# Eleven staging slots for a gathered matrix, and a main loop written out

## The reference

```
XW    = X @ W
s_col = XW @ a[0, :f];  s_row = XW @ a[0, f:]
Z1    = leaky_relu(s_row[:, None] + s_col[None, :], 0.01)
den   = exp(Z1)
num   = A @ den
att   = where(num != 0, den / num, 0)
H     = A @ (att @ XW)
out   = layernorm(X + H)
```

## Time and profile before

| | |
|---|---|
| median of 3 runs | 449.73 us (449.41 to 450.17) |
| profiled execution | 446.65 us |
| its span, first to last instruction | 444.9 us |
| busy in the span | PE 306.8, DVE 280.6, ACT 198.0, POOL 185.5 us |
| mean granted clock of TensorE | 0.843 of full speed |
| loading A, from the first gather to the last matmul of the sums | 57.6 to 186.2 us |
| main loop | 186.5 to about 354 us |
| scatter, second product, layernorm | the rest |

### The profile page before, as it was taken

How to read it: one execution, slowest core, us unless ns; L and a number is a source line. 1 busy time by engine, 2 the same in 40 slices (tenths; PEclk the granted TensorE clock), 3 DMA queues, 4 the chain that set the end, 5 groups by cost and what they waited for, 6 DMA issues and landing times.

```text
span 444.9 us, 5604 instructions
## 1 busy us (share of the span) xinstructions
PE 306.8 (69%) x1466; PEld 145.4 (33%) x1467; DVE 280.6 (63%) x469; ACT 198.0 (45%) x308; POOL 185.5 (42%) x164
## 2 busy tenths in 40 slices
PE   4863214756276456689999999999999720499950
PEld 2563102622123222334434343434344310144420
DVE  0669987277689434499899998966999800201026
ACT  1210030153586233587777787757788820100020
POOL 4000022456878775476455554524555376000000
PEclk9965555886576697999999999999999985699985
DMA  3030042534255566100000000000000041300002
GB/s 117 0 96 2 1 141 71 164 96 122 97 161 158 157 185 196 60 0 1 0 1 0 0 0 0 0 0 0 0 0 1 0 141 47 94 1 0 1 24 71
DMA packets 13439, 24.58 MB, mean 55 GB/s; under 512 B 1648, under 2 KB 8176, under 8 KB 13296
## 3 DMA queue, kind: packets, MB, share of 16 engines
q0 software_dynamic: 5632, 18.88, 13.9%
q1 hardware_dynamic: 7792, 5.50, 4.2%
HBM read 21.23 MB, written 3.15 MB: 55 GB/s over the span
## 4 chain that ended last, share of the span: by engine, by line
PE 49%; DVE 20%; POOL 13%; issue 9%; DMA 5%; ACT 3%; POOLq 0%; SPq 0%; DVEq 0%; ACTq 0%
PE ps L399 17%; PE ps L368 12%; PE ps L428 10%; POOL stage L225 4%; POOL Alo L235 3%; POOL d_b L279 3%; PE ps L394 3%; POOL xws L251 2%; DVE D L574 2%; DMA stage<-adjT,perm 2%; PE ps L301 2%; DVE Alo L744 2%; DVE D L576 2%; PE ps L358 1%; DVE crow L767 1%
## 5 line engine op out<-in xcount | busy, mean ns | idle before, releaser
L269 POOL TENSOR_TENSOR crow<-rrow,cj 128x512 f32<-128x512 f32 x64 | 79.9, 1250 | 76.8 <-DVE crow L767 75.8
L358 PE MATMUL ps<-Ahi,E 128*96 128x512 f16 x128 | 54.6, 484 | 56.3 <-DVE Alo L744 30.0
L399 PE MATMUL ps<-Ahi,D 128*128 x248 | 86.7, 380 | 3.0 <-issue 1.4
L770 DVE TENSOR_TENSOR tmp<-crow,tmp 128x512 f32<-128x512 f32 x64 | 64.4, 1007 | 18.1 <-ACT tmp L508 16.6
L225 POOL DMA_INDIRECT stage<-adjT,perm x32 | 37.3, 1164 | 92.0 <-DVE rs L603 51.8
L368 PE MATMUL ps<-stage,xwp 128*128 128x512 f32 x128 | 70.4, 632 | 1.5 <-DVE stage L757 1.5
L744 DVE TENSOR_TENSOR Alo<-stage,Ahi 128x1024 f16<-128x1024 f32 x24 | 35.5, 1488 | 35.2 <-ACT Ahi L452 35.1
L428 PE MATMUL ps<-Ahi,D 128*128 128x512 f16 x128 | 39.7, 388 | 25.3 <-DVE D L782 25.3
L506 ACT ACTIVATE tmp<-ps 128x512 f32<-128x512 f32 x64 | 38.1, 595 | 37.3 <-PE ps L401 37.3
L452 ACT CAST Ahi<-stage 128x1024 f16<-128x1024 f32 x32 | 33.2, 1042 | 48.2 <-DMA stage<-adjT,perm 47.7
L767 DVE SCALAR_TENSOR_TENSOR crow<-crow 128x512 f32<-128x512 f32 x64 | 49.9, 779 | 0.0
(11 more groups left out here) (158 smaller groups left out, 345.5 us busy)
## 6 DMA issues: line engine op xcount, KB each, us to landing
tmp<-xT SPq DMA_DIRECT2D x1, 1024.0 KB, 4.9
d_xw<-stage SPq DMA_DIRECT2D x1, 1024.0 KB, 5.1
xws<-d_b SPq DMA_DIRECT2D x2, 512.0 KB, 4.7
out<-crow SPq DMA_DIRECT2D x4, 256.0 KB, 2.3
stage<-adjT,perm POOLq DMA_INDIRECT x32, 4.8
xws<-d_xw,perm POOLq DMA_INDIRECT x16, 3.5
d_b<-crow,ranku POOLq DMA_INDIRECT x16, 2.3
stage<-wT SPq DMA_DIRECT2D x1, 64.0 KB, 1.8
```

The source lines that it names most:

```text
L269: nc.gpsimd.tensor_tensor(q_t[c % 2], rrow[:, c * W:(c + 1) * W], cj[:, u:u + 1].to_broadcast([P, W]), ALU.add).then_inc(S["q_ready"], 1)
L358: mm = nc.tensor.matmul(ps[0:R, c, :], E[:, e, b, :], a[:, b, c * W:(c + 1) * W], start=(b == 0 and i == 0), stop=(b == NB - 1 and i == 2))
L399: nc.tensor.matmul(num[c], D[:, d, bass.ds(slot, 1), :], a[:, bass.ds(k, 1), c * W:(c + 1) * W], start=False, stop=(i == 2), skip_group_ch ...
L770: V.tensor_tensor(L_t[c], lz_t[c % 2], L_t[c], ALU.subtract).then_inc(S["sub_done"], 1)
```

## The change

- The ring has eleven slots. Three are in `stage` as before; eight are row blocks 12 to 15 of Ahi and Alo, each read as 1024 float32 columns while it is empty. Gather n + 11 waits for residual n. Casts and residuals from n = 24 on write where slots were, so they wait until the residuals that read those slots are done (`wait_vacated`). The wait for the store of XW moves from the first gather to the eighth.
- Every third residual (n = 2, 5, ..., 29) is POOL's, ten in all, not every fourth.
- The gathers of XW stand at n = 21 to 28, two at each.
- In the main loop POOL does nothing. ACT makes r01 = 0.01 x rrow once, in two instructions; DVE makes the columns shift = -0.99 x score and ebias. The leaky relu is now max(r01 + shift, rrow) in one DVE instruction from two tiles, and the column score goes into the bias of the exp. DVE does it one chunk ahead.
- The loops over pairs are written out on all engines. Only the loop over k is left. The first product of a chunk is split in two halves of 256 columns, the second of which ends the accumulation; the matmul with zeros is gone. PE reads XW directly, and ACT's copies of it (L502) are gone.

```diff
-XWG = 6
-LOS = 4
+XWG = 21
+LOS = 3
+LATE = 12
...
-        st = [stage[:, g * H:(g + 1) * H] for g in range(NG)]
-        q_t = [crow[:, 0:W], crow[:, W:2 * W]]
-        lz_t = [crow[:, 2 * W:3 * W], crow[:, 3 * W:4 * W]]
+        late = [a[:, b, :].bitcast(F32) for b in range(LATE, NB) for a in (Alo, Ahi)]
+        ring = late[1:] + [stage[:, g * H:(g + 1) * H] for g in range(NG)] + late[:1]
+        RG = len(ring)
+        lz_t = [crow[:, i * W:(i + 1) * W] for i in range(2)]
+        r01 = [stage[:, 0:H], crow[:, H:N]]
...
+        def wait_vacated(engine, n, part):
+
+            if n // 2 >= LATE:
+                wait_lo(engine, n // 2 * 2 - (2 if part is Ahi else 3))
...
-            pool.wait_ge(S["xw_out"], 16)
...
-                if n >= NG:
-                    wait_lo(pool, n - NG)
+                if n == RG - NG - 1:
+                    pool.wait_ge(S["xw_out"], 16)
+                if n >= RG:
+                    wait_lo(pool, n - RG)
...
-            for n in range(NG):
+            for n in range(RG):
                 fetch(n)
             for n in range(2 * NB):
                 b, h = divmod(n, 2)
                 if n % LOS == LOS - 1:
                     pool.wait_ge(S["hi_done"], n + 1)
...
+                    wait_vacated(pool, n, Alo)
...
-                if n + NG < 2 * NB:
-                    fetch(n + NG)
+                if n + RG < 2 * NB:
+                    fetch(n + RG)
...
-                if XWG <= n < XWG + NB:
-
-                    for b in range(n - XWG, n - XWG + 1):
+                if XWG <= n < XWG + NB // 2:
+
+                    for b in range(2 * (n - XWG), 2 * (n - XWG + 1)):
...
+            for J in range(NB):
+                lo, hi1 = ends_of(J)
+                for c in range(NC):
+                    t = J * NC + c
+                    if J == 0:
+                        pe.wait_ge(S["sums_sb"], c + 1)
                     else:
-                        lo, hi1 = lo_next, hi1_next
...
+                        pe.wait_ge(S["att_ready"], t - NC + 1)
+                    o = c * W
+                    nc.tensor.matmul(num[c][:, 0:HW], wgt[0:R, J * P:(J + 1) * P], sums[0:R, o:o + HW],
+                                     start=True, stop=False, skip_group_check=True)
+                    with pe.Fori(lo, hi1) as k:
+                        slot = J + (NB - 1) - k
+                        for d, a in ((0, Ahi), (0, Alo), (1, Ahi)):
+                            nc.tensor.matmul(num[c], D[:, d, bass.ds(slot, 1), :], a[:, bass.ds(k, 1), o:o + W],
+                                             start=False, stop=False, skip_group_check=True)
+                    nc.tensor.matmul(num[c][:, HW:W], wgt[0:R, J * P:(J + 1) * P], sums[0:R, o + HW:o + W],
+                                     start=False, stop=True, skip_group_check=True).then_inc(S["num_ready"], 1)
+                    if t >= LAG:
+                        add_bt(t - LAG)
...
-            act.wait_ge(S["xws_in"], 16 * NB)
+            wait_lo(act, 2 * NB - 1)
+            act.wait_ge(S["d_z"], NS)
+            for h in range(2):
+                nc.scalar.mul(r01[h], rrow[:, h * H:(h + 1) * H], SLOPE).then_inc(S["r01_sb"], 1)
             act.wait_ge(S["d_lo"], len(BATCH))
+            act.wait_ge(S["shift_sb"], 2)
...
+            def lz_of(t):
+                J, c = divmod(t, NC)
+                if t < NC:
+                    dve.wait_ge(S["r01_sb"], c // 2 + 1)
+                if t >= 2:
+                    dve.wait_ge(S["sub_done"], t - 1)
+                V.scalar_tensor_tensor(lz_t[t % 2], r01[c // 2][:, c % 2 * W:(c % 2 + 1) * W], shift[:, J:J + 1], rrow[:, c * W:(c + 1) * W],
+                                       ALU.add, ALU.max).then_inc(S["lz_ready"], 1)
```

More of the change, by code:

```diff
@@ L93, in graph_attention_layernorm @@
         a2s = sb("a2s", [P, 2])
-        xwp = sb("xwp", [P, 2, FEAT])
+        shift = sb("shift", [P, NB])
+        ebias = sb("ebias", [P, NB])
         split = sb("split", [P, 2, NB], U32)
@@ L253, in _ @@
                             in_offset=bass.IndirectOffsetOnAxis(ap=perm[:, 1, 2, b:b + 1], axis=0)).then_inc(S["xws_in"], 16)
[L256 to L274, removed]
             for b in range(NB):
@@ L361, in _, with add_bt @@
                     mm.then_inc(S["p_sums"], 1)
-            def add_bt(J, u, c, first, last):
-                t = J * NC + c
+            def add_bt(t):
+                J, c = divmod(t, NC)
                 if c == 0:
-                    pe.wait_ge(S["xwp_ready"], J + 1)
+                    pe.wait_ge(S["xws_in"], 16 * NB)
                 pe.wait_ge(S["att_ready"], t + 1)
-                nc.tensor.matmul(bt[c], xwp[:, u, :], att[c], start=first, stop=last).then_inc(S["bt_added"], 1)
+                nc.tensor.matmul(bt[c], xws[:, J * FEAT:(J + 1) * FEAT], att[c], start=(J == 0), stop=(J == NB - 1)
+                                 ).then_inc(S["bt_added"], 1)
             pe.wait_ge(S["w_lo"], 1)
@@ L372, in _ @@
             LAG = 3
+            HW = W // 2
             def ends_of(J):
[L376 to L405 removed]
@@ L512, in _ @@
-            pair(0, True)
-            with act.Fori(1, NP2) as p:
-                pair(2 * p, False)
-            exp_of(NB * NC - 1, NC - 1)
+                nc.scalar.activation(L_t[c], L_t[c], ACT.Exp, bias=ebias[:, J:J + 1]).then_inc(S["exp_done"], 1)
+            for t in range(NB * NC):
+                c = t % NC
+                act.wait_ge(S["num_ready"], t + 1)
+                if t >= NC:
+                    act.wait_ge(S["att_ready"], t - NC + 1)
+                nc.scalar.activation(L_t[c], num[c], ACT.Square, scale=1.0 / 256).then_inc(S["sq_done"], 1)
+                act.wait_ge(S["sq_done"], t + 1)
+                nc.scalar.activation(L_t[c], L_t[c], ACT.Ln, bias=epst[:, 1:2]).then_inc(S["ln_done"], 1)
+                if t:
+                    exp_of(t - 1)
@@ L754, in att_of @@
+            def att_of(t):
+                c = t % NC
                 dve.wait_ge(S["exp_done"], t + 1)
[L755 removed]
+                if t >= NC:
                     dve.wait_ge(S["bt_added"], t - NC + 1)
                 V.scalar_tensor_tensor(att[c], num[c], 1.0 / 256, L_t[c], ALU.mult, ALU.mult).then_inc(S["att_ready"], 1)
[L759 to L772 removed]
@@ L774, in _ @@
-            pair(0, True)
-            with dve.Fori(1, NP2) as p:
-                pair(2 * p, False)
-            att_of(NB * NC - 1, NC - 1, False)
+            lz_of(0)
+            for t in range(NB * NC):
+                c = t % NC
+                if t + 1 < NB * NC:
+                    lz_of(t + 1)
+                dve.wait_ge(S["lz_ready"], t + 1)
+                dve.wait_ge(S["ln_done"], t + 1)
+                V.tensor_tensor(L_t[c], lz_t[t % 2], L_t[c], ALU.subtract).then_inc(S["sub_done"], 1)
+                if t:
+                    att_of(t - 1)
```

104 lines of the change are left out of this document (24 added, 80 removed).

## The result

The changed kernel takes 432.61 us (median of 4 runs, 432.18 to 432.89) against 449.95 us before in the same session: a ratio of 0.961, interval 0.960 to 0.963. The forecast was 440.8 with a range of 433 to 447: the direction is right, the gain of 17.3 us is almost twice the 8.9 foretold. The profiled execution took 432.18 us, its span is 430.4, 14.5 us under the 444.9 of before. The traces can account for these 14.5; the other 2.8 of the 17.3 come from that the profiled execution of before took 446.65 us where the median is 449.95, and no trace shows where the other executions spend the difference.

A forecast was written before the change was run, and what follows sets the result against it. Loading A was taken as bound by a chain of latencies, the main loop by PE. Span 444.9 - 8.1 + 1.0 - 1.8 = 436.0 us; applied to the median, 449.73 - 8.9 = 440.8 us, range 433 to 447.

The forecast's parts named there:

- Part 1: Loading of A with eleven slots: DMA waits go, copy of crow 3.1 us earlier, batches end at 138.7 us.
- Part 2: End of loading, gathers of XW moved late in POOL's queue: sums end at 178.1 us, a gain of 8.1 us.
- 16 x (0.95 + 0.30) = 20.0: POOL's tail of loading: sixteen gathers of XW at their median, each with a pause, in us; upper end 34.2.
- Rival 3: POOL's tail, sixteen gathers ahead of residual 29, outweighs the rest: slower, 454.5 us; chance 0.07.
- Part 3: Loading, ten residuals on POOL instead of eight: hidden until half block 20, then counted in the tail's sum.
- Part 4: Main loop written out: r01 costs 1.0 us before it, the loop gains 1.8 us, bounds 0 and 4.
- There are two loads per J before and after, so I leave them: 0.: Main loop, PE's step at a new row block: 0.60 us more for two register loads, taken as unchanged.
- Rival 1: Main loop: PE's queue runs ahead when written out, all sixteen stalls go, 9.6 us more, 431.2 us; chance 0.13.
- The sign that was to make Part 4 wrong: Middle of the main loop: a step under 2.4 us, where products 2.48 us apart were foretold.
- The closing matmul with the zero tile took no time on that chain ... : 0: Main loop, end of each chunk's accumulation: replacing that matmul by two halves of 256 columns changes nothing, 0 us.
- Rival 4: Main loop: written-out code stalls in instruction fetch, 9.6 us lost, 450.4 us, no change; chance 0.05.
- Rival 2: Loading: nothing earlier before the tail, batches end at 143.6 us as before; gain 4.0 us, 445.7 us; chance 0.13.

The follow-up runs named there:

- e15_every_fourth: The changed kernel with every fourth residual on POOL (eight) instead of every third; 429.39 us, ratio 0.957.
- e7_r01_first: The changed kernel with ACT's two r01 instructions moved ahead of the four copies of the sums; 431.96 us, ratio 0.962.
- e1: The kernel before with only the loading changed (eleven slots, POOL's order, every third residual) and the old main loop; 443.96 us, ratio 0.989.
- e9: The changed kernel with PE alone back in its loop over pairs, the odd row block's bounds loaded a chunk ahead; 443.88 us, ratio 0.988.

## Why the prediction was right or wrong

**Part 1, right.** The copy of crow at 84.66 (85.8 foretold), slots at 103.7 (104.5), first batch at 114.0 (115.0), end of the batches at 137.7 (138.7). ACT's waits for gathers of A are 5.4 us in all. The limit of this part is not the data, as said.

**Part 2, the mechanism right, its sizes off.** POOL's last gather of A ended at 146.6 (145.7 foretold), and from there POOL worked without a gap to residual 29 at 175.5 (173.1 foretold). The term "16 x (0.95 + 0.30) = 20.0" was 17.8 us of gathers and not 15.2, 2.6 more: four of them took 1.20, 1.50, 1.80 and 1.96. The kernel before had already shown this price: its sixteen gathers of XW took 18.4 us in all, a mean of 1.15 and not the median of 0.952. A sum of many needs the mean. The pauses were 1.2 us less, for behind a residual a gather of XW came after 0.16 us and not 0.8. PE's last three half blocks took 6.8 and not 5.0, with the clock at 0.50 from 176 to 181 us. With 7.4 us to the first product (7.5 foretold) it starts at 189.8 where the text said 185.6: 2.9 us earlier than before, where 8.1 - 1.0 = 7.1 stood. With the old loop behind it, and so without r01, the loading part gained 4.0 us at the first product and 5.5 by the medians, where 8.1 stood. Rival 3 named the right place, and the early gathers show how much lay in it: 12.75 us. It did not turn the sign.

The Trainium skill, "SBUF — State Buffer", "Who interferes with whom", says that a tensor_tensor leaves descriptor writing alone, with the reason marked as inferred, and by it none of these gathers is stretched. The trace disagrees. These are POOL's and DVE's instructions around the two dearest gathers (start us, us, line, operation, idle before):

```profile
165.50 1.80 POOL L260 DMA_INDIRECT xws<-d_xw,perm  x1 [0.30 <-issue]
167.61 0.94 POOL L260 DMA_INDIRECT xws<-d_xw,perm  x1 [0.30 <-issue]
168.86 1.96 POOL L260 DMA_INDIRECT xws<-d_xw,perm  x1 [0.30 <-issue]
```

```profile
165.26 1.23 DVE L718 TENSOR_TENSOR Alo<-Ahi 128x1024 f16<-128x1024 f32 x1 [7.89 <-ACT Ahi L432]
167.64 2.36 DVE L718 TENSOR_TENSOR Alo<-stage,Ahi 128x1024 f16<-128x1024 f32 x2 [1.16 <-ACT Ahi L432]
```

A gather that starts while DVE subtracts ends 0.81 us after DVE does: 166.49 to 167.30, 170.00 to 170.82. The one that starts first (167.61 against 167.64) is not touched. Those of 1.20 and 1.50 fit in the same way, and so do four in the run with every fourth residual (1.97, 1.80, 1.96 and 1.80). My own reason for the median was that DVE is mostly idle there. It is, but these four gathers fell on the few instructions that it has, and that is the 2.6 us.

**Part 3, hidden up to half block 20, and in the tail not.** Every fourth residual likely saves some 3 us, for which the forecast had no term of its own: it had the three residuals in the sum of the tail and did not ask which of them the other spacing would leave there.

**Part 4, the failed step.** In the prediction's words: "There are two loads per J before and after, so I leave them: 0." The loads stayed and their stops went. Before, they cost 7.6 us in all (what eleven steps of the chain have over their neighbours, 0.5 to 1.5 each); after, one stop of 0.97 is left, at the row block behind the one with three steps of k. The reason stood in none of the steps: PE's instruction queue, with 21.0 us a pair, paced the loop of before, and not the matmuls. Written out, it needs less than they do. Rival 1 is what happened, given 0.13 and priced at 9.6. The sign that was to make Part 4 wrong came too: steps of 2.38, under 2.4.

With it goes "The closing matmul with the zero tile took no time on that chain ... : 0". It was right for the kernel before, where taking it out gains 0.6 us that can't be told from nothing, and wrong for the kernel after, where it costs 5.75. That matmul was free as long as the queue set the pace. Sum from the chains, from the first product to the 54th: 53 x 0.10 = 5.3 us of closings, 7.6 - 1.0 of stops and 0.3 of two slightly long steps before, less 2.6 us of the slow start after, 9.6 of the 10.0 measured. The rest of the loop gives the other 1.4, as the 1.3 of the forecast said, though ACT sets the pace there (1.84 us a chunk) and not DVE (2.15 foretold).

Of Part 4's other terms: DVE's subtraction is at 691 ns without stretched ones (0.69 foretold), the leaky relu took 742 ns and not 680, and neither is on the path. Rival 4 did not occur: behind the loop's start no step of the written-out code is longer than its neighbours except the one at 293 us, and the four with three steps of k. Rival 2 did not either. The Trainium skill, "Runtime: NRT & Kernel Launch", "Instruction fetch mechanics", says that a taken branch stalls the fetch when its target lies outside the pages at hand; the 2.3 to 2.6 us per pair that the outer loop adds may hold a cost of that kind, but no run separates it. The same section gives about 200 ns per register for loads that the runtime itself puts in; here a load of a bound from the on-chip table takes 0.68 to 0.75 us of PE's queue, and the measurement decides.

**Chances.** Faster by over 0.2% had 0.89 and happened. Of the 8.2 us between 440.8 and 432.61, the loop gave 9.6 us more than its 1.8, the loading 4.2 us less than its 7.1, and 2.8 come from the last step of the sum, which kept 3.1 us between the profiled execution and the median where there were 0.4. The first two partly hide each other. That the result lies only 0.4 us below the range is luck in part: with the loading as forecast it would have been over 4 us below. It missed because rival 1 was given 0.13, though a step that is longer where the loads stand was the one thing that the chain showed plainly.

## What to carry to other kernels

Where a busy engine's chain shows pauses named "issue", add up its time over a full turn of the loop, then take a little work away: if the turn stays the same and no wait for another engine fills it, the engine's instruction queue is the bound, and no instruction's price can be read off the gaps. Count register loads there at 0.7 us each, and see whether writing the loop out gives the queue its lead back. A piece of 0.00 us in a chain is not free; look at what the piece behind it takes without it. Work that nobody needs yet still has a place in a queue: put it where that engine waits anyway, not ahead of what others wait for.

## What the runs showed of the hardware that was not expected

- A load of one register from the on-chip table takes 0.68 us of PE's queue (48 more loads, 32.8 us; 0.75 by the medians). At a fixed address in the loop over pairs the stops are the same as at one from a register.
- PE's outer loop costs its queue 2.3 to 2.6 us per turn of eight chunks, besides the loads (an estimate: 21.0 us a pair against 18.4 to 18.7 written out).
- A closing matmul of one column ahead of a float32 product costs 0.09 to 0.10 us a time (5.75 us for 64; steps of 2.49 and 2.38), and shows as 0.97 against 0.86 us of that product.
- A gather of XW that POOL starts while DVE runs a tensor_tensor ends 0.81 us after that instruction does (four here, four in `e15_every_fourth`); one that started 0.03 us ahead of it was not touched.
- TensorE's clock fell to its lower level at the start of the loop in the kernels where PE had waited 2.3 to 3.4 us ahead of the first product, with one exception: after 2.74 us in `e7_r01_first` it stayed at 1.00, where after 2.74 us in `e15_every_fourth` it fell. So the length of that wait alone does not decide. Where it had waited 0.51 (before), 0.83 (e1) or 1.78 us (e9) it did not fall. The first two steps are 4.77 and 2.59 us with the fall (changed kernel) and 3.70 and 2.38 without (e7): 1.3 us.
